# Softmax denominators in two attentions: three key tiles summed by accumulating transfers, four adds on Pool, one part left for TensorE

## The reference, cut to what matters

```
sim  = einsum('bhdi,bhdj->bhij', q, k) * scale + bias     # first: bias from a small network
attn = softmax(sim);  out = einsum('bhij,bhdj->bhdi', attn, v)
...
weights = softmax((qk + qe) / sqrt(d_head))               # second: relative-position term qe
output  = einsum('bhqk,bhkd->bhqd', weights, v)
```

## Time and profile before

| | us |
|---|---|
| median of three runs | 2824.24 (2823.91 to 2826.27) |
| the profiled execution's own time | 2824.42 |
| its span in the profile | 2822.6 |
| TensorE busy | 2467.3 (87%) |
| VectorE busy | 1989.9 (70%) |
| Pool busy | 1967.6 (70%) |
| ScalarE busy | 1403.2 (50%) |

### The profile page before, as it was taken

How to read it: one execution, slowest core, us unless ns; L and a number is a source line. 1 busy time by engine, 2 the same in 40 slices (tenths; PEclk the granted TensorE clock), 3 DMA queues, 4 the chain that set the end, 5 groups by cost and what they waited for, 6 DMA issues and landing times. The chain is left out here.

```text
span 2822.6 us, 47289 instructions
## 1 busy us (share of the span) xinstructions
PE 2467.3 (87%) x18516; PEld 822.8 (29%) x18516; DVE 1989.9 (70%) x3075; ACT 1403.2 (50%) x2548; POOL 1967.6 (70%) x763
## 2 busy tenths in 40 slices
PE   7799999999999999968998999999999999660355
PEld 2464222222222222225552222222222222240234
DVE  4475778778778778627886878788787878278234
ACT  3344555555555655623335666666566666450112
POOL 3123888888888888844445888888888888740773
PEclk9899999999999999989999999999999999885657
DMA  4994222232221232029764233222322231170347
GB/s 80 235 239 146 50 50 50 54 80 60 51 52 50 50 80 64 9 101 278 247 228 142 50 92 70 65 49 72 98 58 64 50 85 29 61 224 0 93 129 257
DMA packets 236268, 278.16 MB, mean 99 GB/s; under 512 B 65393, under 2 KB 171377, under 8 KB 232843
## 3 DMA queue, kind: packets, MB, share of 16 engines
q1 hardware_dynamic: 225548, 249.89, 32.6%
q0 software_dynamic: 6144, 16.85, 1.9%
q10 hardware_dynamic: 4352, 8.39, 0.8%
HBM read 165.17 MB, written 110.67 MB: 98 GB/s over the span
## 5 line engine op out<-in xcount | busy, mean ns | idle before, releaser
L854 POOL TENSOR_TENSOR room_af<-room_af 128x2048 f32<-128x2048 f32 x160 | 725.5, 4535 | 164.2 <-ACT room_af L826 150.4
L1225 POOL TENSOR_TENSOR bias<-bias 128x2048 f32<-128x2048 f32 x160 | 724.6, 4529 | 133.2 <-ACT bias L1195 114.4
L826 ACT ACTIVATE room_af<-PS 128x512 f32<-128x512 f32 x1024 | 555.9, 594 | 396.7 <-PE PS L748 396.7
L635 DVE CUSTOM_DVE_ANT_0 PS<-PS,bias 128x1024 f32<-128x1024 f32 x512 | 620.0, 1241 | 163.1 <-PE PS L623 143.1
L1195 ACT ACTIVATE bias<-PS 128x512 f32<-128x512 f32 x1024 | 555.7, 594 | 356.0 <-PE PS L1123 354.6
L1004 DVE TENSOR_REDUCE row_min_kf<-PS 128x1 f32<-128x1024 f32 x512 | 603.7, 1219 | 120.4 <-PE PS L996 115.5
L741 PE MATMUL PS<-QS_af,KS_af 128*128 128x512 f16 x1024 | 334.5, 387 | 14.3 <-PEq L90 4.5
L1118 PE MATMUL PS<-stacks_kf 128*128 128x512 f16 x1024 | 334.9, 387 | 12.6 <-PEq L90 8.5
L774 PE MATMUL PS<-room_af,V_af 128*32 128x512 f32 x2048 | 273.2, 605 | 1.2 <-ACT room_af L826 1.2
L1143 PE MATMUL PS<-bias,V_kf 128*32 128x512 f32 x2048 | 272.7, 605 | 1.2 <-ACT bias L1195 1.2
L748 PE MATMUL PS<-turned_bias,eyes 64*32 64x512 f16 x4096 | 210.6, 388 | 0.0
(11 more groups left out here) (184 smaller groups left out, 2973.4 us busy)
## 6 DMA issues: line engine op xcount, KB each, us to landing
query_key_halves<-bias SPq DMA_DIRECT2D x32, 768.0 KB, 4.0
query_key_halves<-room_af SPq DMA_DIRECT2D x32, 512.0 KB, 4.3
stacks_kf<-query_key_halves SPq DMA_DIRECT2D x64, 256.0 KB, 7.9
KS_af<-query_key_halves SPq DMA_DIRECT2D x48, 256.0 KB, 4.9
QS_af<-query_key_halves SPq DMA_DIRECT2D x48, 256.0 KB, 6.9
lows_kf<-query_key_halves SPq DMA_DIRECT2D x96, 128.0 KB
token_rows<-rows_t SPq DMA_DIRECT2D x16, 514.0 KB, 4.3
FT_t<-token_rows SPq DMA_DIRECT2D x16, 514.0 KB, 5.6
```

What stands on the lines that cost most here:

```text
L635: nc.vector.tensor_tensor_reduce(out=max_ps[n % len(max_ps)], in0=max_ps[n % len(max_ps)], in1=bias_h[:, g * HG + j, z:z + N], scale=-1.0, ...
L826: nc.scalar.activation(prob[:, n % PR, head, :], score_ps[s % 3], ACT.Exp).then_inc(exps, 1)
L854: nc.gpsimd.tensor_tensor(acc[:, u % 2], so_far, prob[:, n % PR], ALU.add).then_inc(acc_ok, 1)
L1225: nc.gpsimd.tensor_tensor(acc[:, u % 2], so_far, prob[:, n % PR], ALU.add).then_inc(acc_ok, 1)
```

## The change

In both attentions the tiles of a unit are summed in another way. The ring has six tiles and holds tiles 1 to 7 of a unit. Tile 0 is written straight into `sums[u % 2]`. Tiles 1, 2 and 3 (`MOVED = 3`) are added to it by accumulating transfers that Pool issues (`dma_start(..., accum_op=ALU.add)`), each of which waits for the one before. Pool adds tiles 4 to 7 in `acc` with three adds, and with a fourth (`add_sums`) adds `acc` to `sums`. The denominators then have one part, `sums`. Those of the last unit have four: `sums`, `acc` (tiles 4 and 5) and tiles 6 and 7.

The order moves too: the denominators of a unit come at step 4 of the next, not step 1; the reciprocals behind them; the finish of unit u comes at step 2 of unit u + 2 (`BACK = 2`), the store one unit later than before. The lists of row maxima in the first attention are shifted so that the step of the denominators has the fewest. In the first attention `sums` and `acc` lie in the half of the tile `bias` that isn't used there, and the ring fills the room that ring and sums had; in the second `sums` is a tile of its own. The second attention is changed as the first; its copies of the functions are left out below.

```
-                PR = 4
-                prob = room[:, 0:o1].rearrange("p (r j n) -> p r j n", r=PR, j=HG)
-                acc = room[:, o1:o2].rearrange("p (r j n) -> p r j n", r=2, j=HG)
+                PR = 6
+                o1, o2 = PR * HG * CH, H * ZU * W // 2
+                ring = room[:, 0:o1].rearrange("p (r j n) -> p r j n", r=PR, j=HG)
+                sums = zf[:, o2:o2 + 2 * HG * CH].rearrange("p (r j n) -> p r j n", r=2, j=HG)
+                acc = zf[:, o2 + 2 * HG * CH:o2 + 3 * HG * CH].rearrange("p (j n) -> p j n", j=HG)
...
-                ADDS = KTU - 3
+                MOVED = 3
+                ADDS = KTU - 1 - MOVED
+                STEPS = KTU - 1
+                FIN, BACK = 2, 2
+                def prob(n):
+                    u, kt = divmod(n, KTU)
+                    return sums[:, u % 2] if kt == 0 else ring[:, (u * STEPS + kt - 1) % PR]
...
-                EARLY = ((), (1,), (), (), (), (), (11,), ())
-                LATE = ((0,), (2, 3), (4, 5), (6,), (7, 8), (9, 10), (12, 13), (14, 15))
-                DEN = 1
+                EARLY = ((), (1,), (), (), (), (), (), (13,))
+                LATE = ((0,), (2, 3), (4, 5), (6, 7), (8, 9), (10, 11), (12,), (14, 15))
+                DEN = 4
...
                             def denominators(n, u):
                                 pe.wait_ge(max_read, n - 1)
-                                pe.wait_ge(acc_ok, ADDS * (u + 1))
-                                parts = [prob[:, (KTU * u + kt) % PR] for kt in range(ADDS + 1, KTU)] + [acc[:, u % 2]]
+                                if u < NU - 1:
+                                    pe.wait_ge(acc_ok, ADDS * (u + 1))
+                                    parts = [sums[:, u % 2]]
+                                else:
+                                    pe.wait_ge(moved, 16 * MOVED * (u + 1))
+                                    pe.wait_ge(acc_ok, ADDS * u + 1)
+                                    parts = [sums[:, u % 2], acc] + [prob(KTU * u + kt) for kt in range(MOVED + 3, KTU)]
...
-                                if n >= PR and j == 0:
-                                    u, kt = divmod(n - PR, KTU)
-                                    act.wait_ge(weighed, n - PR + 1)
-                                    if kt <= ADDS:
-                                        act.wait_ge(acc_ok, ADDS * u + max(kt, 1))
+                                u, kt = divmod(n, KTU)
+                                if kt == 0 and j == 0 and u >= 2:
+                                    act.wait_ge(max_full, job_at[(u - 2, "den")] + 1)
+                                if kt >= 1 and j == 0 and u * STEPS + kt - 1 >= PR:
+                                    u, kt = divmod(u * STEPS + kt - 1 - PR, STEPS)
+                                    act.wait_ge(weighed, KTU * u + kt + 2)
+                                    if kt < MOVED:
+                                        act.wait_ge(moved, 16 * (MOVED * u + kt + 1))
                                     else:
-                                        act.wait_ge(max_full, job_at[(u, "den")] + 1)
+                                        act.wait_ge(acc_ok, ADDS * u + max(kt - MOVED, 1))
...
+                            def move_tile(n):
+                                u, kt = divmod(n, KTU)
+                                pool.wait_ge(exps, HG * (n + 1))
+                                if kt == 1:
+                                    pool.wait_ge(weighed, KTU * u + 1)
+                                if MOVED * u + kt >= 2:
+                                    pool.wait_ge(moved, 16 * (MOVED * u + kt - 1))
+                                nc.gpsimd.dma_start(sums[:, u % 2].rearrange("p j n -> p (j n)"), prob(n).rearrange("p j n -> p (j n)"),
+                                                    accum_op=ALU.add).then_inc(moved, 16)
...
+                            def add_sums(u):
+                                pool.wait_ge(moved, 16 * MOVED * (u + 1))
+                                pool.wait_ge(acc_ok, ADDS * (u + 1) - 1)
+                                nc.gpsimd.tensor_tensor(sums[:, u % 2], sums[:, u % 2], acc, ALU.add).then_inc(acc_ok, 1)
...
                             for n in range(NU * KTU):
-                                add_tile(n)
-                                if n % KTU == ADDS and n >= KTU:
-                                    finish(n // KTU - 1)
-                            finish(NU - 1)
+                                u, kt = divmod(n, KTU)
+                                if kt == 1:
+                                    move_tile(n)
+                                    if u >= 1:
+                                        add_sums(u - 1)
+                                if kt == FIN:
+                                    if u >= BACK:
+                                        finish(u - BACK)
+                                    move_tile(n)
+                                if kt == MOVED + 2:
+                                    move_tile(n - 2)
+                                if kt == MOVED + 2 or kt > MOVED + 2 and u < NU - 1:
+                                    add_tile(n)
+                            for u in range(NU - BACK, NU):
+                                finish(u)
```

More of the change, by code:

```diff
@@ L910, in attention_keys_first @@
                 max_row = tile("max_row", [HG * TT, 2, P], F16)
[L912 to L915, removed]
+                PR = 6
+                o1, o2 = HG * CH * PR, HG * CH * (PR + 1)
+                ring = zf[:, 0:o1].rearrange("p (r j n) -> p r j n", r=PR, j=HG)
+                acc = zf[:, o1:o2].rearrange("p (j n) -> p j n", j=HG)
+                sums = tile("sums", [P, 2, HG, CH], F32)
                 rec = zf[:, o2:o2 + 2 * CH].rearrange("p (r n) -> p r n", r=2)
@@ L1222, in add_tile @@
-                                if kt >= 2:
-                                    pool.wait_ge(acc_ok, ADDS * u + kt - 1)
-                                so_far = prob[:, (n - 1) % PR] if kt == 1 else acc[:, u % 2]
-                                nc.gpsimd.tensor_tensor(acc[:, u % 2], so_far, prob[:, n % PR], ALU.add).then_inc(acc_ok, 1)
-                            for n in range(NU * KTU):
-                                add_tile(n)
-                                if n % KTU == FIN and n >= KTU:
-                                    finish(n // KTU - 1)
@@ L1231, in _, with add_sums @@
-                            finish(NU - 1)
+                                if done >= 1:
+                                    pool.wait_ge(acc_ok, done)
+                                nc.gpsimd.tensor_tensor(acc, prob(n - 1) if first else acc, prob(n), ALU.add).then_inc(acc_ok, 1)
+                            def add_sums(u):
+                                pool.wait_ge(moved, 16 * MOVED * (u + 1))
+                                pool.wait_ge(acc_ok, ADDS * (u + 1) - 1)
+                                nc.gpsimd.tensor_tensor(sums[:, u % 2], sums[:, u % 2], acc, ALU.add).then_inc(acc_ok, 1)
```

91 lines of the change are left out of this document (54 added, 37 removed).

## The result

The changed kernel takes 3088.01 us (3087.31 to 3091.36, 4 runs) against 2824.8 on the same chip: ratio 1.093, 95% interval 1.092 to 1.095. I had 2892 us and a range to 3085: the direction was right, the size (+68 forecast, +263 measured) was not, and the time lies just outside the range.

What follows compares the result with a forecast made beforehand. Pool, waiting for its own transfers, was to bound each unit instead of TensorE: +28 and +47 us in the two attentions, less 7 for initial air, net +68 on 2824.42, giving 2892 us; range of 8 in 10, 2730 to 3085.

Steps and rivals of the forecast that it cites:

- TensorE's floor: Unit length if TensorE kept the pace with 1.80 us less denominator work: 28.44 and 27.24 us, a gain of 110 us.
- The landing: Accumulating 1024 KB transfer, from end of issue until landed: 5.9 us, with its data counted twice plus 1.5 us fixed.
- The issue: Pool's time to issue one accumulating transfer: 1.13 us, three a unit making 3.4 us.
- Pool's chain: Pool's four adds, finish, three issues and one exposed landing per unit: 31.1 us in the first attention, 30.6 in the second.
- the delay by other transfers: Load bursts every second unit, meeting tile 1's transfer and seldom tile 2's: costed at nothing.
- the cover of 7.9 us: An add and a finish on Pool between the transfers of tiles 1 and 2, said to hide the first landing.
- Rival C: Load bursts slow tile 2's transfer by some 4 us in half the units: +124 us, about 3015; chance 0.10.
- the starts and ends of the attentions: Pool's initial air saves 7 us over both attentions; the tail is set at nothing, +-3 us.
- Pool's idle time: Sign: Pool idle about 6 us a unit in front of tile 3's transfer, released by a transfer.
- Odd and even units: Sign of the load-burst rival: idle time before tile 3's transfer differs between even and odd units.
- TensorE's wait in front of the denominators: Sign: TensorE idle 2.5 to 3.5 us a unit before the denominators, released by Pool's add.
- about 4.5 us of air per unit: Pool's spare time per unit in the kernel before the change, beside a full TensorE.

Runs made afterwards that it cites:

- small moves: Changed kernel with its three accumulating transfers cut to 128 of 2048 columns (64 KB, not 1024 KB); ratio 0.966, periods 28.71 and 27.27 us.
- the single edits: Each alone on the changed kernel: tile 3's transfer issued behind Pool's first add, ratio 1.065; row maxima issued a step earlier, ratio 1.073.
- both: Changed kernel with tile 3's transfer behind Pool's first add and row maxima a step earlier, together; ratio 1.009, periods 29.46 and 30.34 us.

## Why the prediction was wrong

- TensorE's floor was right: 28.44 and 27.24 us forecast, 28.71 and 27.27 with small moves.
- The landing was right within its parts: 6.9 us from the start of the issue forecast (1.03 + 5.9), 7.0 to 7.1 measured, by counting the data twice. The issue holds Pool for 0.57 us until its next instruction starts, not 1.13; the add behind it is 0.3 slower.
- Pool's chain was right: 31.1 and 30.6 forecast, 31.23 and 30.35 where it stands alone. Alone it gives the ratio 1.034; I had 1.024. The agreement is partly luck: cheaper issues make up for a wait of 7.5 us from the start of move 2 to that of move 3, where I had 7.0.
- What failed is one step of the sum, the delay by other transfers, which I set at nothing: "The other traffic is a burst of loads every second unit [...]. I cost it at nothing and keep it as a rival." Two things were in it. The row maxima's transfers weren't in "the other traffic" at all, though each unit's scores start with them. SyncE issues them at step 6, and the diff has move 3 at step 5, behind the landing of move 2, which by my own chain is step 6, so they meet. On top of the chain of the forecast their delay costs 2.5 and 2.6 us a unit (33.75 against 31.23, 32.92 against 30.35). And the bursts do meet move 1 (11.7 us instead of 7.1), which the cover of 7.9 us doesn't hide; on top of the maxima that adds 0.0 and 0.6 us a unit, and without the maxima 1.4 and 2.5. Together the step is 2.5 and 3.2 us a unit, 178 us where the sum has 0. Rival C had looked for them at move 2 and gave it 0.10.
- The clock had no term. I took TensorE's waits as waits. From 262 to 1330 us it is busy 919.91 us, while the same stretch before had 922.7 with 56 us (31 x 1.80) more of work at full clock: 53 us lost at the half level; in the second attention 58 (916.36 against 914.35 less 56). Together 111 us, as much as the denominators had saved. Small moves runs the same 17540 matrix instructions as the changed kernel and keeps TensorE busy for 2371.0 us against 2488.5 in the whole program: 118 us, by another way.
- The account by waits: -111 denominators, +179 maxima, +58 Pool's sum, +111 clock = +237. The windows that it is read from grew by 232 (1068 and 1054 us against 968 and 922). By periods it is 31 x (33.75 - 30.24 + 33.56 - 29.04) = +249, of the 263 measured. The other 14 lie at the starts and ends of the attentions, where I had -7 and nothing; no run breaks them down. The share of the clock isn't a cost of its own that another change could take away, since each slow stretch comes behind a pause.
- Of the signs that I had named, Pool's idle time (6.6 us) and the landing came true. Odd and even units differed too, but in front of move 2, not of move 3. TensorE's wait in front of the denominators, which I expected in every unit (2.5 to 3.5 us), came 7 times in the first attention and 9 times in the second (16.7 and 40.8 us); it became the rule only once the maxima were out of the way.
- One reading was off without consequence: "about 4.5 us of air per unit" on Pool. The terms that I used give 30.24 - 5 x 4.64 - 3.27 = 3.8 us and 29.04 - 5 x 4.64 - 2.70 = 3.1.

What stays open: why a small transfer waits up to 3 us for its turn. The traces show that the small ones pass between the packets of a move and not only behind it, but not by what order an engine picks its next packet. The collision is shown by issuing the maxima earlier and by making the moves small; no run moved the maxima's transfers to another queue.

## What to carry to other kernels

A transfer of 1 MB that is put beside the work must be set against every small transfer on whose landing an engine waits, at the moment at which both are issued; its mean share of the DMA engines (0.68 here) says nothing of that. Where TensorE is full, a wait costs it more than its length: here 237 us of waits came with 111 us lost at the half clock. And where two loops have nearly the same length, undo them together before giving either up: here the single edits gave 2.6% and 1.8%, both 7.7%. A mean period can hide two kinds of units; look at a few in a row.

## What the runs showed of the hardware that I had not expected

- Accumulating 1024 KB inside SBUF: 7.0 to 7.1 us to landing and 5.2 us of all 16 engines; a plain copy from the same queue 4.6 and 2.7; 64 KB accumulated, 2.4 us to landing.
- A direct transfer issued by Pool has a row of 0.87 us (0.55 plain), but Pool's next add starts 0.57 us after its start and then lasts 0.3 us longer than usual.
- TensorE waited up to 5.0 us for four 1 KB transfers beside one accumulating megabyte, though they come from another queue.
- Each pause of TensorE of more than 3 us in the two attentions of the changed kernel was followed by 3 to 7 us at the half clock (0.54 in the window from 718 us); the mean from 700 to 1100 us then reads 0.92.
